# Router logits on fp32r passes turned by VectorE, and attention rows turned through DRAM

## Chip, cores and metric

The kernel runs on one core of one Trainium2 chip. The time is the device time of one execution in microseconds, the median of three runs.

## What is computed

A block of the macaron kind: a half-weighted mixture of experts, linear attention without softmax, and the same mixture again. The input is 4 sequences of 1024 rows of 128 values.

```python
x = L0_attn_x
x = x + 0.5 * ffn(layernorm(x))      # router, 16 experts of 128, top 4 of the best 2 groups, 2 shared experts
x = x + attention(layernorm(x))      # 32 heads of 4, group norm over each head and sequence, output matrix
x = x + 0.5 * ffn(layernorm(x))      # same weights as the first

logits = x_flat @ router_w.T                       # 16 logits a row
scores = sigmoid(logits); s = scores + bias        # choice by s, weights by scores
h = einsum('td,edf->etf', x, gate_w); u = einsum('td,edf->etf', x, up_w)
y = einsum('etf,efd->etd', silu(h) * u, down_w)
routed = einsum('etd,te->td', y, combine)
```

All of it is float32.

## The kernel before

**Steps and units.** The 4096 rows are cut into 8 blocks of 512, and each goes through the mixture twice: 16 steps. A step has 18 units (2 shared experts and 16 routed ones), and two steps form a pair, unrolled as `pair(p, ...)` on each engine, with `u` from 0 to 35, `w = u % 18` the place in the step and `s = u // 18` the half. Pairs 2 to 5 (steps 4 to 11) also carry the attention of one sequence each, as small pieces (`attention_stage(u, b)`) hung onto given units. Semaphores order the engines; each engine works off its own queue in order.

**One unit.** A product in float32 accuracy is made of three passes in fp32r (`product`, L509 to L516): high part of the weights times high part of the rows, low times high, high times low. A unit is three such products: gateP, upP, and yP for the unit four places earlier, so nine passes with 512 columns. ScalarE then applies silu to gateP in place (L902), VectorE multiplies it by the routing weight CB into T (L1239) and that by upP into A (L1270), ScalarE rounds A to A_hi (L876), and GpSimd forms A_lo = A - A_hi (L396). gateP and upP have two banks each: TensorE may write gateP of unit n+2 only when T of unit n is there (`gate_left`, L256), and upP when A of unit n is there.

**The next step's rows.** The normalised rows XN of step t+2 are stored to DRAM (`store_rows`), loaded in 32x32 squares into XB (`load_squares`), and at place 16 VectorE turns each square (`turn_rows`, L1153), which gives XT, the rows' transpose. XT_hi is rounded by ScalarE at place 1 (`next_high`), XT_lo is formed by GpSimd at place 2 (`next_low`), and TensorE needs both at place 0 of the next step.

**Router.** At place 1 of step t TensorE forms the logits of step t+1 in full float32: four matmuls with 128 columns of XT as the weights and the 16 columns of RT moving (`logits`, L540 to L556), into backP, with the rows on the partitions. VectorE's `route` follows in eight parts at places 2 to 9, with `route_silu` on ScalarE at place 3. `next_stats` on VectorE is at place 1, the turning of the output (`turn_output`) at place 5, of the weights at place 10. SP stores them and loads them again as CB, spread over the partitions (`load_weights`). ScalarE copies the finished sum yP to YT at place 4 (`copy_y`) before TensorE begins the next sum.

**Attention.** XA holds the normalised rows of a sequence (ScalarE, units 5 to 8). At unit 9 TensorE forms XA'XA (L571) and transposes four tiles of XA into backP, at unit 14 the other four (L585); ScalarE copies them to XAT at units 10 and 15 (L846). XAT is used at unit 33, as the weights of the last product. Small products and VectorE's work on them lie between, at units 11 to 32.

Of the kernel before, what the change touches and what calls it, by code (L numbers as in the profile page):

```python
# [34 lines left out]
P = 128  # L35
# [13 lines left out]
def macaron_kernel(nc, x, Wqkv_w, Wqkv_b, gn_w, gn_b, out_w, out_b, router_w, bias,  # L49
# [23 lines left out]
    ATT_ACT = 11  # L73
# [7 lines left out]
    with ctx:  # L81
# [63 lines left out]
        RT = sb("RT", [P, E])  # L145
        ebias = sb("ebias", [P, E])
# [21 lines left out]
        XAT = sb("XAT", [P, BT, P])  # L168
# [11 lines left out]
        quad = sb("quad", [P, P])  # L180
# [10 lines left out]
        Bm = P1  # L191
        brow = Mf
# [13 lines left out]
        y_rows = nc.dram_tensor("y_rows", [STEPS, BLOCK, P], F32, kind="Internal").ap()  # L206

# [17 lines left out]
        logits_done, silu_route, route_seq = sem("logits_done"), sem("silu_route"), sem("route_seq")  # L225
        norm_seq = sem("norm_seq")
# [11 lines left out]
        xa_ready = sem("xa_ready")  # L238
        attended = sem("attended")
# [29 lines left out]
        def _(sp):  # L269
# [78 lines left out]

            def store(t):
# [35 lines left out]
        def _(pool):  # L385
# [66 lines left out]
            def pair(p, first, attention, last):  # L452
                n = PAIR * p
                for u in range(PAIR):
                    w, s = u % UNITS, u // UNITS
                    early = first and s == 0
                    if early and u in SPLIT_AT:
                        split_low(SPLIT_AT[u])
                    if first and u == 24:
# [5 lines left out]
                    if w == 2 and not early and not (last and s == 1):  # L465
# [43 lines left out]
        def _(pe):  # L509
# [30 lines left out]
            def logits(t):  # L540

                pe.wait_ge(xt_ready, t + 1)
                if t >= 1:

                    pe.wait_ge(route_seq, ROUTE_OPS * (t - 1) + 2)
# [4 lines left out]
                if t % 2 == 0 and 0 <= b < BATCH:  # L550

                    pe.wait_ge(att_act, ATT_ACT * b + 5)
# [11 lines left out]
            def attention_stage(u, b):  # L564
# [9 lines left out]
                if u in (9, 14):  # L574

                    g = (u - 9) // 5
                    if g == 0:

                        pe.wait_ge(attended, 2 * (b + 1))
                        pe.wait_ge(route_seq, ROUTE_OPS * (2 * (b + ATT0) + 1) + 2)  # L580
                    else:

                        pe.wait_ge(att_act, ATT_ACT * b + 2)
                    for j in range(TILES):
                        mm = pe.transpose(backP[:, j * P:(j + 1) * P], XA[:, g * TILES + j, 0:P], ident[:, :])  # L585
                    mm.then_inc(att_pe, 1)
                if u == 14:

                    pe.wait_ge(att_act, ATT_ACT * b + 4)
# [12 lines left out]
                if u == 21:  # L602
                    pe.wait_ge(att_act, ATT_ACT * b + 7)
# [9 lines left out]
                if u == 30:  # L613
                    pe.wait_ge(att_act, ATT_ACT * b + 10)
                    pe.matmul(attP[:, 0:P], ATs[:, :], WoT[:, :], start=True, stop=True)  # L615
                    pe.matmul(attP[:, P:2 * P], zb[:, :], WoT[:, :], start=True, stop=True).then_inc(att_pe, 1)
                if u == 33:
                    pe.wait_ge(att_act, ATT_ACT * b + 11)
                    for g, bank in enumerate((attP, backP)):
                        if g == 0:  # L620
# [144 lines left out]
        def _(act):  # L765
# [56 lines left out]
            def attention_stage(u, b):  # L822
# [10 lines left out]
                if u == 10:  # L833
                    act.wait_ge(att_pe, 12 * b + 1)
# [8 lines left out]
                if u in (10, 15):  # L843
                    g = (u - 10) // 5
                    act.wait_ge(att_pe, 12 * b + 2 + g)
                    act.copy(XAT[:, g * TILES:(g + 1) * TILES, :], backP[:, :]).then_inc(att_act, 1)  # L846
                if u == 20:
                    act.wait_ge(att_pe, 12 * b + 6)
# [549 lines left out]
```

## Time and profile before

| | |
|---|---|
| median of 3 runs | 654.15 us (654.02 to 654.58) |
| profiled execution | 654.32 us, its span 652.6 us |
| TensorE busy | 646.5 us, 99% |
| TensorE weight loads busy | 536.4 us, 82% |
| VectorE busy | 527.4 us, 81% |
| ScalarE busy | 400.2 us, 61% |
| GpSimd busy | 464.1 us, 71% |
| granted TensorE clock | full through the whole span |

A row in order of time shows the start, the duration, the engine, the line, the operation, what it writes and what it reads, the shape and how many instructions were merged; in brackets stands the idle time of the engine before it. Matmuls are pipelined: 0.39 us is the length of one, not the distance between two. The span begins at 0; step t's place w lies at unit 18t + w. Steps 4 and 5 form the first attention pair.

### The profile page before, as it was taken

How to read it: one execution, taken by the hardware profiler on the slowest of the kernel's cores; microseconds unless marked ns; L12 is line 12 of the kernel's file. 1: busy time of each engine (PE TensorE's matmuls, PEld its weight loads, DVE VectorE, ACT ScalarE, POOL GpSimd, SP SyncE). 2: the span in 40 equal slices, each digit the busy share in tenths (PEclk: the TensorE clock that was granted, in tenths of full speed). 3: DMA queues.
4: the chain of work that ended last, by engine and by line, in shares of the span. 5: the costliest groups of instructions: out<-in, count | busy, mean ns of one | idle time of the engine just before them, and what ended most of it. 6: DMA issues, size and time to landing. Idle time of an engine off the chain costs nothing.

```text
span 652.6 us, 10128 instructions
## 1 busy us (share of the span) xinstructions
PE 646.5 (99%) x3043; PEld 536.4 (82%) x3043; DVE 527.4 (81%) x1468; ACT 400.2 (61%) x790; POOL 464.1 (71%) x400
## 2 busy tenths in 40 slices
PE   8999999999999999999999999999999999999997
PEld 7888888888888888888888888888878888888886
DVE  6898879797886979879798788897887978778674
ACT  4876656566675556755658556585565656655554
POOL 6997776777866678566785667866678677767664
PEclk9999999999999999999999999999999999999999
DMA  8726352816236162271532814528146282633510
GB/s 235 273 61 260 88 237 51 275 33 198 95 82 244 33 181 113 62 264 33 157 138 50 274 22 124 198 49 264 43 104 225 49 262 63 190 125 101 203 32 33
DMA packets 107542, 90.07 MB, mean 138 GB/s; under 512 B 67408, under 2 KB 89824, under 8 KB 107488
## 3 DMA queue, kind: packets, MB, share of 16 engines
q1 hardware_dynamic: 107488, 89.43, 43.5%
q8 instruction: 24, 0.39, 0.2%
q14 instruction: 30, 0.25, 0.1%
HBM read 79.45 MB, written 9.96 MB: 137 GB/s over the span
## 4 chain that ended last, share of the span: by engine, by line
PE 98%; DVE 1%; issue 0%; ACT 0%; POOL 0%; DVEq 0%; POOLq 0%
PE gateP L512 10%; PE yP L516 10%; PE yP L512 10%; PE yP L513 10%; PE upP L512 10%; PE gateP L516 10%; PE upP L516 10%; PE gateP L513 10%; PE upP L513 10%; PE backP L554 2%; PE attP L571 1%; PE yP L639 1%; PE attP L624 1%; PE backP L624 1%; PE backP L585 1%; PE attP L615 0%
## 5 line engine op out<-in xcount | busy, mean ns | idle before, releaser
L396 POOL TENSOR_TENSOR A_lo<-A,A_hi 128x512 fp32r<-128x512 f32 x287 | 370.7, 1293 | 171.5 <-ACT A_hi L876 170.8
L902 ACT ACTIVATE gateP<-gateP 128x512 f32<-128x512 f32 x252 | 146.5, 581 | 178.4 <-PE gateP L516 177.6
L1239 DVE TENSOR_TENSOR T<-gateP,CB 128x512 f32<-128x512 f32 x252 | 172.9, 686 | 83.4 <-ACT gateP L902 81.5
L876 ACT CAST A_hi<-A 128x512 fp32r<-128x512 f32 x287 | 176.3, 614 | 28.9 <-DVE A L1270 24.2
L1270 DVE TENSOR_TENSOR A<-upP,T 128x512 f32<-128x512 f32 x254 | 175.7, 692 | 8.7
L512 PE MATMUL gateP<-XT_hi,W_hi 128*128 128x512 f32 x288 | 117.5, 408 | 0.0
L512 PE MATMUL yP<-A_hi,W_hi 128*128 128x512 f32 x288 | 112.5, 391 | 0.0
L516 PE MATMUL yP<-A_lo,W_hi 128*128 128x512 f32 x288 | 112.4, 390 | 0.0
L516 PE MATMUL gateP<-XT_lo,W_hi 128*128 128x512 f32 x288 | 112.4, 390 | 0.0
L513 PE MATMUL gateP<-XT_hi,W_lo 128*128 128x512 f32 x288 | 112.3, 390 | 0.0
L513 PE MATMUL yP<-A_hi,W_lo 128*128 128x512 f32 x288 | 112.1, 389 | 0.0
L512 PE MATMUL upP<-XT_hi,W_hi 128*128 128x512 f32 (+1 forms) x286 | 111.7, 391 | 0.0
L516 PE MATMUL upP<-XT_lo,W_hi 128*128 128x512 f32 (+1 forms) x286 | 111.4, 389 | 0.0
L513 PE MATMUL upP<-XT_hi,W_lo 128*128 128x512 f32 (+1 forms) x286 | 111.2, 389 | 0.0
L512 PEld LDWEIGHTS upP<-XT_hi,W_hi 128*128 128x128 f32 x286 | 53.7, 188 | 13.4 <-DVE A L1270 1.9
L516 PEld LDWEIGHTS gateP<-XT_lo,W_hi 128*128 128x128 f32 x288 | 54.1, 188 | 11.8
L512 PEld LDWEIGHTS gateP<-XT_hi,W_hi 128*128 128x128 f32 x288 | 54.2, 188 | 11.5 <-DVE T L1239 1.6
L516 PEld LDWEIGHTS yP<-A_lo,W_hi 128*128 128x128 f32 x288 | 54.1, 188 | 11.5
L512 PEld LDWEIGHTS yP<-A_hi,W_hi 128*128 128x128 f32 x288 | 54.1, 188 | 11.5 <-POOL A_lo L396 0.2
L513 PEld LDWEIGHTS yP<-A_hi,W_lo 128*128 128x128 f32 x288 | 54.1, 188 | 11.2
L516 PEld LDWEIGHTS upP<-XT_lo,W_hi 128*128 128x128 f32 x286 | 53.7, 188 | 11.5
L513 PEld LDWEIGHTS upP<-XT_hi,W_lo 128*128 128x128 f32 x286 | 53.7, 188 | 10.8
(225 smaller groups left out, 627.8 us busy)
## 6 DMA issues: line engine op xcount, KB each, us to landing
CB<-combT SPq DMA_DIRECT2D x126, 512.0 KB, 6.8
y_rows<-YB SPq DMA_DIRECT2D x60, 64.0 KB, 1.9
YP<-y_rows SPq DMA_DIRECT2D x15, 256.0 KB, 2.8
x_rows<-XN SPq DMA_DIRECT2D x13, 256.0 KB, 2.3
XB<-x_rows SPq DMA_DIRECT2D x52, 64.0 KB, 2.3
out_dram<-X SPq DMA_DIRECT2D x7, 256.0 KB, 5.0
X<-in_L_attn_x_dram SPq DMA_DIRECT2D x3, 512.0 KB, 9.5
W_in<-in_L_ffn_gate_w_dram SPq DMA_DIRECT2D x4, 256.0 KB, 4.8
```

Of the source, the lines that this page charges most:

```text
L396: pool.tensor_tensor(A_lo[:, slot, :], A[:, slot, :], A_hi[:, slot, :].bitcast(F32), ALU.subtract).then_inc(low_done, 1)
L512: pe.matmul(dst, hi_w, hi_x, start=start, stop=False)
L513: pe.matmul(dst, lo_w, hi_x, start=False, stop=False)
L516: return pe.matmul(dst, hi_w, lo_x, start=False, stop=stop)
L554: mm = pe.matmul(backP[:, j * E:(j + 1) * E], XT[:, j * P:(j + 1) * P], RT[:, :], start=True, stop=True)
L571: mm = pe.matmul(attP[:, 0:P + 1], XA[:, j, 0:P], XA[:, j, :], start=(j == 0), stop=(j == BT - 1))
L585: mm = pe.transpose(backP[:, j * P:(j + 1) * P], XA[:, g * TILES + j, 0:P], ident[:, :])
L624: mm = pe.matmul(bank[:, j * P:(j + 1) * P], XAT[:, g * TILES + j, :], Bm[:, :], start=True, stop=True)
L876: act.copy(A_hi[:, v % SLOTS, :], A[:, v % SLOTS, :]).then_inc(high_done, 1)
L902: act.activation(dst, gateP[u % 2][:, :], ACT.Silu).then_inc(silu_done, 1)
L1239: dve.tensor_tensor(T[:, u % TS, :], silu, weights, ALU.mult).then_inc(gate_weighted, 1)
L1270: dve.tensor_tensor(A[:, u % SLOTS, :], bank[:, :], gated, ALU.mult).then_inc(mul_done, 1)
```

## The change

The router's matrix is split into a high and a low part once, RT4, with 128 columns: four copies of the 16 experts, each with its two parts side by side. In steps 2 to 15 RT4 is TensorE's weights, and XT_hi and then XT_lo move past it, 512 columns each, summed in backP. The result has (copy, expert, part) on the partitions and the rows along the free axis. A new `turn_logits` on VectorE at place 1 turns it: four transpositions of 32x128, each out of one group of 32 partitions and the tiles' matching 32 columns, and a sum over the two parts into prepP, from which `route` goes on. Because the logits now read XT_hi and XT_lo, `next_high` and `next_low` move to place 0, ahead of A_hi and A_lo. Steps 0 and 1 keep the old logits.

The transposes of XA leave TensorE and the copies leave ScalarE. SP stores XA to DRAM and loads it in 32x32 squares into a part of W_in, which is free by then, and VectorE turns each half of it at units 29 and 30 into XAT, another part of W_in. The other lines adapt counts (ATT_ACT, ATT_PE) and let quad share Gn's place.

```diff
+        RT4 = sb("RT4", [P, P // SQUARE, E, 2], F32R)
...
+            def store_attention_rows(b):
+                sp.wait_ge(xa_ready, b + 1)
+                sp.dma_start(xa_rows[b].rearrange("(j p) d -> p j d", p=P),
+                             XA[:, :, 0:P]).then_inc(xa_stored, 16)
...
+                squares = xa_rows[b].rearrange("(m c) (b r) -> b c m r", c=SQUARE, r=SQUARE)
+                for i in range(P // SQUARE):
+                    sp.dma_start(XAB[i * SQUARE:(i + 1) * SQUARE, :].rearrange("c (m r) -> c m r", r=SQUARE),
+                                 squares[i]).then_inc(xa_in, 16)
...
                 turn_output(t - 1)
+                attention = t % 2 == 0 and ATT0 <= t // 2 < ATT1
+                if attention:
+                    store_attention_rows(t // 2 - ATT0)
                 if t + 2 < STEPS:
                     store_rows(t + 2)
                 if t + 1 < STEPS:
                     spread_weights(t + 1)
                 if t + 2 < STEPS:
                     load_squares(t + 2)
+                if attention:
+                    load_attention_squares(t // 2 - ATT0)
                 if t + 1 < STEPS:
                     load_weights(t + 1)
...
+                    if first and u == 13:
+
+                        pool.wait_ge(router_split, 1)
+                        pool.tensor_tensor(RT4[:, :, :, 1], RT[:, :].unsqueeze(1).broadcast_to([P, P // SQUARE, E]),
+                                           RT4[:, :, :, 0].bitcast(F32), ALU.subtract).then_inc(router_split, 1)
...
-                    if w == 2 and not early and not (last and s == 1):
+                    if w == 0 and not early and not (last and s == 1):
                         next_low(2 * p + s + 1, (s + 1) % 2)
...
-                for j in range(TILES):
-                    mm = pe.matmul(backP[:, j * E:(j + 1) * E], XT[:, j * P:(j + 1) * P], RT[:, :],
-                                   start=True, stop=True)
-                mm.then_inc(logits_done, 1)
+                router = RT4[:, :, :, :].rearrange("p a e i -> p (a e i)")
+                pe.wait_ge(xt_hi_ready, t + 1)
+                pe.matmul(backP[:, :], router, XT_hi[:, t % 2, :], start=True, stop=False)
+                pe.wait_ge(xt_lo_ready, t + 1)
+                pe.matmul(backP[:, :], router, XT_lo[:, t % 2, :], start=False, stop=True).then_inc(logits_done, 1)
...
-                    for j in range(TILES):
-                        mm = pe.transpose(backP[:, j * P:(j + 1) * P], XA[:, g * TILES + j, 0:P], ident[:, :])
-                    mm.then_inc(att_pe, 1)
...
-                    act.copy(XAT[:, g * TILES:(g + 1) * TILES, :], backP[:, :]).then_inc(att_act, 1)
...
+                    if w == 0 and not first and not (last and s >= 1):
+                        next_high(t0 + s + 1, (s + 1) % 2)
...
-                        if w == (6 if early else 1):
-                            next_high(t0 + s + 1, (s + 1) % 2)
+                        if first and u in (6, UNITS):
+                            next_high(s + 1, (s + 1) % 2)
...
+            def turn_logits(t):
+
+                dve.wait_ge(logits_done, t + 1)
+                for a in range(P // SQUARE):
+                    group = slice(a * SQUARE, (a + 1) * SQUARE)
+                    own = backP[group, :].rearrange("p (j a c) -> p a j c", j=TILES, c=SQUARE)[:, a]
+                    ins = dve.transpose(lgT[group, :].rearrange("p (j c) -> p j c", c=SQUARE), own)
+                ins.then_inc(logits_turned, 1)
+                dve.wait_ge(logits_turned, t - 1)
+                dve.tensor_reduce(prepP[:, 0:TILES * E], lgT[:, :].rearrange("p (k i) -> p k i", i=2), AX.X,
+                                  ALU.add).then_inc(logits_summed, 1)
...
+                if u in (29, 30):
+                    g = u - 29
+                    dve.wait_ge(xa_in, 64 * (b + 1))
+                    dve.transpose(XAT[:, g * TILES:(g + 1) * TILES, :].rearrange("p j d -> p (j d)"),
+                                  XAB[:, g * BLOCK:(g + 1) * BLOCK]).then_inc(xat_ready, 1)
...
+                        if w == 1 and not early:
+                            turn_logits(t0 + s + 1)
```

## Rows read from the trace of the kernel before

**Rows 1.** The page: the chain that ended last, shares by engine.

```profile
PE 98%; DVE 1%; issue 0%; ACT 0%; POOL 0%; DVEq 0%; POOLq 0%
```

**Rows 2.** In order of time: start, duration, instruction; places 1 to 3 of step 4.

```profile
164.74 0.39 PE L512 MATMUL gateP<-XT_hi,W_hi 128*128 128x512 f32 x1
...
166.42 0.67 DVE L1270 TENSOR_TENSOR A<-upP,S 128x512 f32<-128x512 f32 x1
...
166.78 0.96 PE L554 MATMUL backP<-RT,XT 128*128 128x16 f32 x8
...
167.59 0.49 PE L512 MATMUL gateP<-XT_hi,W_hi 128*128 128x512 f32 x1
...
169.20 0.69 DVE L1239 TENSOR_TENSOR T<-gateP,CB 128x512 f32<-128x512 f32 x1 [0.64 <-ACT gateP L902]
...
169.77 0.39 PE L512 MATMUL gateP<-XT_hi,W_hi 128*128 128x512 f32 x1
...
169.93 0.69 DVE L1270 TENSOR_TENSOR A<-upP,T 128x512 f32<-128x512 f32 x1
...
170.53 0.22 DVE L1058 TENSOR_SCALAR near<-backP 128x64 f32<-128x64 f32 x1
...
172.77 0.68 DVE L1239 TENSOR_TENSOR T<-gateP,CB 128x512 f32<-128x512 f32 x1
```

**Rows 3.** In order of time, step 3: T of 3.2, T of 3.6, gateP of 3.8.

```profile
131.53 0.69 DVE L1239 TENSOR_TENSOR T<-gateP,CB 128x512 f32<-128x512 f32 x1 [1.27 <-ACT gateP L902]
...
140.46 0.68 DVE L1239 TENSOR_TENSOR T<-gateP,CB 128x512 f32<-128x512 f32 x1
...
142.30 0.39 PE L512 MATMUL gateP<-XT_hi,W_hi 128*128 128x512 f32 x1
```

**Rows 4.** In order of time, step 4: T of 4.6 and gateP of 4.8.

```profile
179.38 0.68 DVE L1239 TENSOR_TENSOR T<-gateP,CB 128x512 f32<-128x512 f32 x1
...
180.12 0.50 PE L512 MATMUL gateP<-XT_hi,W_hi 128*128 128x512 f32 x1
```

**Rows 5.** In order of time, step 5: places 1, 2, 7, 9 and 12.

```profile
208.10 0.68 DVE L1270 TENSOR_TENSOR A<-upP,S 128x512 f32<-128x512 f32 x1
...
208.48 0.96 PE L554 MATMUL backP<-RT,XT 128*128 128x16 f32 x8
...
209.73 0.48 PE L512 MATMUL gateP<-XT_hi,W_hi 128*128 128x512 f32 x1
...
211.32 0.69 DVE L1239 TENSOR_TENSOR T<-gateP,CB 128x512 f32<-128x512 f32 x1 [1.66 <-ACT gateP L902]
...
224.05 0.68 DVE L1239 TENSOR_TENSOR T<-gateP,CB 128x512 f32<-128x512 f32 x1
...
224.78 0.50 PE L512 MATMUL gateP<-XT_hi,W_hi 128*128 128x512 f32 x1
...
233.79 0.69 DVE L1239 TENSOR_TENSOR T<-gateP,CB 128x512 f32<-128x512 f32 x1 [0.73 <-ACT gateP L902]
```

**Rows 6.** Waits: who waited for whom, us in total, times, longest.

```profile
PEld gateP L512 <- DVE T L1239: 1.6, 4, 0.4
```

**Rows 7.** The chain that ended last, in order of time: place 9 of step 4.

```profile
186.38 0.44 PE backP L585 x4
```

**Rows 8.** Groups by line: count, busy us, mean ns of one, idle time before.

```profile
L420 POOL TENSOR_TENSOR XT_lo<-XT,XT_hi 128x512 fp32r<-128x512 f32 x14 | 18.2, 1298 | 0.0
...
L1158 DVE STREAM_TRANSPOSE XT<-XB 128x512 f32<-128x512 f32 x13 | 9.1, 702 | 0.0
...
L1099 DVE TENSOR_REDUCE prepP<-ahead 128x16 f32<-128x128 f32 x16 | 4.7, 295 | 0.5
...
L1145 DVE STREAM_TRANSPOSE CTB<-comb 128x64 f32<-128x64 f32 x14 | 3.3, 235 | 0.0
```

**Rows 9.** SP's queue in order of time, step 4; the page's issues of XB.

```profile
193.66 10.97 SPq L319 DMA_DIRECT2D CB<-combT  x8
...
XB<-x_rows SPq DMA_DIRECT2D x52, 64.0 KB, 2.3
```

More of the change, by code:

```diff
@@ L72, in macaron_kernel @@
     ATT_OPS = 18
-    ATT_ACT = 11
+    ATT_ACT = 9
+    ATT_PE = 10
     assert D == P and BT * P == SEQ and NBLK == 2 * BATCH and E == GROUPS * PER_GROUP
@@ L167, in macaron_kernel @@
         XA = sb("XA", [P, BT, P + 1])
-        XAT = sb("XAT", [P, BT, P])
+        lgT = sb("lgT", [P, P])
         GS = sb("GS", [P, P + 1])
@@ L191, in macaron_kernel @@
         Bm = P1
+        quad = Gn
+        XAB = W_in[:, 0:3, :, :].rearrange("p u i d -> p (u i d)")[:, 0:BT * P]
+        XAT = W_in[:, 3:6, :, :].rearrange("p u i d -> p (u i) d")[:, 0:BT, :]
         brow = Mf
@@ L206, in macaron_kernel @@
         y_rows = nc.dram_tensor("y_rows", [STEPS, BLOCK, P], F32, kind="Internal").ap()
+        xa_rows = nc.dram_tensor("xa_rows", [BATCH, SEQ, P], F32, kind="Internal").ap()
         x_first, x_rest = sem("x_first"), sem("x_rest")
@@ L238, in macaron_kernel @@
         xa_ready = sem("xa_ready")
+        xa_stored, xa_in, xat_ready = sem("xa_stored"), sem("xa_in"), sem("xat_ready")
         attended = sem("attended")
@@ L347, in load_squares, with load_attention_squares @@
                                  squares[b]).then_inc(rows_in, 16)
+            def store_attention_rows(b):
+                sp.wait_ge(xa_ready, b + 1)
+                sp.dma_start(xa_rows[b].rearrange("(j p) d -> p j d", p=P),
+                             XA[:, :, 0:P]).then_inc(xa_stored, 16)
+            def load_attention_squares(b):
+                sp.wait_ge(xa_stored, 16 * (b + 1))
+                if b == 0:
+                    sp.wait_ge(w_lo_done, UNITS)
+                else:
+                    sp.wait_ge(xat_ready, 2 * b)
+                squares = xa_rows[b].rearrange("(m c) (b r) -> b c m r", c=SQUARE, r=SQUARE)
+                for i in range(P // SQUARE):
+                    sp.dma_start(XAB[i * SQUARE:(i + 1) * SQUARE, :].rearrange("c (m r) -> c m r", r=SQUARE),
+                                 squares[i]).then_inc(xa_in, 16)
             def store(t):
@@ L540, in logits @@
             def logits(t):
-                pe.wait_ge(xt_ready, t + 1)
-                if t >= 1:
-                    pe.wait_ge(route_seq, ROUTE_OPS * (t - 1) + 2)
+                if t < 2:
+                    pe.wait_ge(xt_ready, t + 1)
+                    if t == 1:
+                        pe.wait_ge(route_seq, 2)
+                    for j in range(TILES):
+                        mm = pe.matmul(backP[:, j * E:(j + 1) * E], XT[:, j * P:(j + 1) * P], RT[:, :],
+                                       start=True, stop=True)
+                    mm.then_inc(logits_done, 1)
+                    return
+                if t == 2:
+                    pe.wait_ge(router_split, 2)
+                    pe.wait_ge(route_seq, ROUTE_OPS + 2)
+                else:
+                    pe.wait_ge(logits_turned, t - 2)
                 b = (t - 1) // 2 - ATT0
@@ L573, in attention_stage @@
                     mm.then_inc(att_pe, 1)
[L574 to L583, printed above, removed]
-                    for j in range(TILES):
-                        mm = pe.transpose(backP[:, j * P:(j + 1) * P], XA[:, g * TILES + j, 0:P], ident[:, :])
-                    mm.then_inc(att_pe, 1)
                 if u == 14:
-                    pe.wait_ge(att_act, ATT_ACT * b + 4)
+                    pe.wait_ge(att_act, ATT_ACT * b + 3)
                     pe.matmul(attP[:, 0:P], GS[:, 0:P], WvT[:, :], start=True, stop=True)
@@ L905, in pair @@
                             split_high(unit)
+                    if first and u == 6:
+                        act.wait_ge(setup_sb, 1)
+                        act.copy(RT4[:, :, :, 0], RT[:, :].unsqueeze(1).broadcast_to([P, P // SQUARE, E])
+                                 ).then_inc(router_split, 1)
                     if first and u == 20:
@@ L1052, in route @@
                 if part == 0:
-                    dve.wait_ge(logits_done, t + 1)
-                    flat = backP[:, 0:TILES * E]
+                    if t < 2:
+                        dve.wait_ge(logits_done, t + 1)
+                        flat = backP[:, 0:TILES * E]
+                    else:
+                        dve.wait_ge(logits_summed, t - 1)
+                        flat = prepP[:, 0:TILES * E]
                     near_f = near[:, :, :].rearrange("p t e -> p (t e)")
```

38 lines of the change are left out of this document (17 added, 21 removed).

## The prediction

> **What bounds the kernel now.** I read the chain that ended last first: it lies on TensorE for 98% of the span [rows 1]. So time is won only by taking slots out of TensorE's queue, and lost only where another engine makes it wait. Then the instructions in order of time. Units are named step.place: 4.6 is place 6 of step 4. A unit is nine passes of 128x512; in 4.1 they begin at 164.74 and what follows them at 166.78 [rows 2], so a unit takes 2.04 us and a pass 0.227 of the queue (its shown 0.39 overlaps its neighbours).
>
> Next the reader should see how near VectorE is. T of 4.2 starts at 169.20, A at 169.93, and A ends at 170.62 [rows 2]: with the gaps a unit takes 1.45 us of VectorE and leaves it 0.59 of 2.04 for everything else. TensorE may not write gateP of unit n+2 before T of unit n is done (gate_left). In step 3, T of 3.6 ends at 141.14 and gateP of 3.8 starts at 142.30, so 1.16 is in hand [rows 3]. In step 4, the first half of an attention pair, T of 4.6 ends at 180.06 and gateP of 4.8 starts at 180.12 [rows 4]: nothing is in hand. In step 5, T of 5.7 ends at 224.73 and gateP of 5.9 starts at 224.78 [rows 5]: nothing either. The waits agree: TensorE's weight loads waited for T four times, once for each attention pair [rows 6].
>
> **What leaves TensorE.** The eight logit matmuls of 128x16 (two records for each of four) take from 166.78 to 167.59, and the unit behind them takes 169.77 - 167.59 = 2.18 in place of 2.04 [rows 2]: 0.81 + 0.14 = 0.95. Two passes of the kind that all units consist of replace them, 0.45, which saves 0.50. Steps 2 to 15 are concerned, so place 1 of steps 1 to 14: six steps without attention (1, 2, 3, 12, 13, 14), four first halves (4, 6, 8, 10) and four second halves. In a second half fp32 matmuls of the attention follow the logits, the slow unit stays and 0.35 is saved. Four transposes of XA take 0.44 [rows 7]; they leave at places 9 and 14, 0.88 in each first half. If nothing waited, the sum would be 6 x 0.50 + 4 x 0.50 + 4 x 0.35 + 4 x 0.88 = 9.9 us.
>
> **What VectorE gets.** turn_logits stands ahead of next_stats, of the attention's statistics and of T of place 2; all of that queues behind its wait, and TensorE behind T. A of 4.1 ends at 167.09. The second new pass starts at 164.74 + 10 x 0.227 = 167.01 and takes 0.39 [rows 2], so the logits are there at 167.40, a wait of 0.31. Then come four transpositions of 32x128. One of 64 columns takes 0.235 and one of 512 takes 0.702 [rows 8]; on that line 128 columns take 0.235 + 64 x 0.00104 = 0.30. How closely the four follow each other isn't in the trace: no instruction of VectorE there works on other partitions than its neighbour. The bounds: overlapping by 0.09, as A does, which ends at 170.62, with what starts at 170.53 [rows 2], they take 4 x 0.21, some 0.89 with the last one's tail; one after the other with 0.04 between, as from T to A of 4.2 [rows 2], they take 4 x 0.34 = 1.36. The pairwise sum that waits for them is like the reduction of 0.295 [rows 8], less such an overlap: 0.21. So turn_logits costs 1.10 or 1.57 behind its wait. I take 1.57: the four write four different groups of partitions, and every overlap in the trace is between instructions on the same ones.
>
> The Trainium skill sides with the long end: "VectorE: DVE Perf Modes", section "Two Vector instructions with no wait between them", says that an instruction whose operands begin in another quadrant of 32 partitions than those before it starts only when all earlier ones have finished. By it the sum is the one with 1.57, without it the one with 1.10. No row here shows it.
>
> **First halves.** From the end of A of 4.1 to T of 4.2 VectorE had 2.11 us, 0.64 of it idle [rows 2], so 1.47 of work. After the change T of 4.2 starts at 167.40 + 1.57 + 1.47 = 170.44, later than 169.20 by 1.24. From there to T of 4.6 VectorE gives nothing back: 2.15 us pass from A of 4.2 to T of 4.3 [rows 2] where a unit leaves 0.59, and the router's parts go on. So TensorE is held at gateP of 4.8 until 1.2 later than before, whatever it saved ahead of it. It will also wait at place 4, since copy_y stands behind A_hi and route_silu in ScalarE's queue, but that lies within the same 1.2. Then it saves 0.88 at places 9 and 14. Net +0.33 each, +1.3 for four.
>
> **Second halves.** The logits of step 5 start at 208.48; + 0.227 + 0.39 they are there at 209.10. A of 5.1 ends at 208.78 and T of 5.2 starts at 211.32 after 1.66 of idle time, so next_stats takes 0.88. With 1.57 and 0.88, T starts at 211.55, behind a gateP that moves from 209.73 to 209.38 [rows 5]: 2.17 behind it in place of 1.59. Places 2 to 5 give VectorE about what a unit leaves, so none pays it back; place 6 adds 1.07 for dev2, and T of 5.7 is about 0.7 later behind its gateP, with 0.05 in hand. A stall of 0.68, less 0.35: +0.33 each, +1.3 for four.
>
> **Other steps.** VectorE idles 1.27 before T of 3.2 [rows 3]. The new work is 0.31 + 1.57 = 1.88 and gateP comes 0.36 earlier, so T falls back by 0.97 behind its gateP; by another 0.14 as the next unit is no longer slow, and by some 0.15 that VectorE idled up to T of 3.6. That is 1.25 where 1.16 is in hand: a stall of 0.1 at place 8, one as large at place 12, and 0.15 at place 4, where copy_y comes after two pieces that follow A of place 2. So 0.35 of the 0.50 goes again. Five steps save 0.15 each. Step 1 saves nothing, where ScalarE still copies XT first and XT_lo comes late. Together -0.75.
>
> **Edits at no cost.** XT_hi and XT_lo move to place 0, ahead of A_hi and A_lo. gateP of 4.0 is whole about 163.6; silu and XT_hi take 0.6 each and XT_lo 1.30 [rows 8], so it is there about 166.1, where the second pass asks for it at 167.01; if it weren't, each logit would wait up to 1.3. A_lo is formed over a unit ahead of its use and bears that. ScalarE loses two copies of XAT, for which nobody waited. VectorE's two transpositions of XAT take 0.702 each [rows 8] less the overlap. They fall to 5.11, where VectorE idles 0.73 before T of 5.12 [rows 5], and to 5.12, where T of 5.13 comes some 0.5 later, far less than the 1.2 in hand in a unit without attention; with no cover they would cost 5 us. On SP's queue the four loads of squares stand ahead of the CB loads, which began at 193.66 and the first of which is wanted by T of 5.2 at 211.32 [rows 5, 9]. The present squares, half as large, land in 2.3 us [rows 9]; the new ones take some 9 of 17 even if each waits for the one before it. XA's store is issued in SP's wait for the normalised rows. The router's two splits are an instruction each in step 0.
>
> **Sum.** 1.3 + 1.3 - 0.75 = +1.85 us. The profiled execution took 654.32 (span 652.6), the median is 654.15; on the median 656.0, slower by 0.28%.
>
> **Rivals.** (a) The four transpositions overlap, 1.10 in all. T of 4.2 is then 0.77 late: first halves 0.74 - 0.88 = -0.14, second halves a stall of 0.25 and -0.1, other steps -0.48: together -3.9, so 650.3. For it: small instructions overlap throughout. Against it: the different partitions. From the forecast to it each 0.1 of turn_logits is 1.2 us of the kernel, so below 1.42 the kernel is faster than before. (b) The waits at 4.8 and 5.9 aren't VectorE's doing, and all 9.9 us are won: 644.3. Against it stand the 0.06 and 0.05 us. (c) A transposition of 128 columns out of PSUM takes 0.075 more than the line says, 0.3 more at each of 14 steps: 659.7. The trace turns only SBUF; but T and A read PSUM and take 0.69, no more than is usual for their size. (d) Something between (a) and the forecast, within 0.2% of before.
>
> **Chances.** Forecast 0.50 (653.5 to 658.5; a fifth of it within 0.2%), (a) 0.20, (b) 0.07, (c) 0.10, (d) 0.13. A measurement of this kernel tells 0.2% (1.3 us) from no change. Faster 0.27, same 0.23, slower 0.50. The range takes in (a) and most of (c): 650.3 to 659.5.
>
> **What would show it.** Right: two logit passes of 0.23 with no slow unit behind; four records of about 0.30 with starts 0.34 apart on VectorE; T of 4.2 some 1.6 us later behind its gateP; TensorE's waits for T grown from 1.6 us to several, at places 8 and 9 of attention steps. Wrong: starts of the four 0.21 apart, waits for T as before, CB or XAT waited for, or XT_lo waited for at each logit.

## The result, and the profile of the changed kernel

The changed kernel takes 656.35 us (median of 7 runs, 656.21 to 656.91). The kernel before, timed beside it, takes 654.16 (7 runs, 653.95 to 654.58). The ratio is 1.0033, 95% interval 1.0022 to 1.0045: slower by 2.2 us, outside the noise of the runs. The forecast was 656.0 and slower by 0.28%.

| | before | after |
| --- | --- | --- |
| profiled execution, us | 654.32 | 656.27 |
| its span, us | 652.6 | 654.5 |
| TensorE busy, us and share of the span | 646.5, 99% | 642.6, 98% |
| TensorE's weight loads waiting for T, us | 1.6 [rows 6] | 7.3 |

The page of the changed kernel: the line of the span, the busy times, and the shares of the chain that ended last, which answer to [rows 1].

```profile
span 654.5 us, 9988 instructions
...
PE 642.6 (98%) x2927; PEld 522.1 (80%) x2927; DVE 554.5 (85%) x1546; ACT 396.9 (61%) x783; POOL 465.0 (71%) x401
...
PE 84%; DVE 12%; issue 2%; POOL 1%; DMA 1%; ACT 1%; SPq 0%; DVEq 0%; ACTq 0%
```

The share of VectorE in the chain went from 1% to 12%. TensorE's busy share, 99% before and 98% now, hardly shows it, as each stall is a few tenths of a microsecond in a step of 42. So I read the waits next. The columns are engine, tile and line, what it waited for, us in total, times, longest.

```profile
PEld gateP L547 <- DVE T L1298: 7.3, 12, 1.0
PEld yP L547 <- ACT YT L819: 3.7, 8, 0.7
...
PE gateP L547 <- DVE T L1298: 2.8, 7, 0.6
PEld attP L640 <- DVE chmean L1254: 2.7, 4, 0.7
...
PEld attP L632 <- DVE Mm L1248: 2.1, 4, 0.5
...
PEld backP L602 <- POOL XT_lo L450: 0.5, 1, 0.5
```

The first line answers to [rows 6]: 4 waits with 1.6 us became 12 with 7.3. YT, chmean and Mm are new among the waits of this size; the forecast has the first and not the other two. XT_lo, which now stands ahead of the logits, was waited for once.

Then the instructions in order of time (start, duration, engine and line, operation; in brackets the idle time ahead and what ended it), places 0 to 5 of step 4. They answer to [rows 2].

```profile
163.89 1.29 POOL L450 TENSOR_TENSOR XT_lo<-XT,XT_hi 128x512 fp32r<-128x512 f32 x1 [0.74 <-ACT XT_hi L844]
...
165.54 0.67 DVE L1329 TENSOR_TENSOR A<-upP,S 128x512 f32<-128x512 f32 x1
...
165.91 0.39 PE L600 MATMUL backP<-XT_hi,RT 128*128 128x512 f32 x1
...
166.14 0.39 PE L602 MATMUL backP<-XT_lo,RT 128*128 128x512 f32 x1
...
166.37 0.40 PE L547 MATMUL gateP<-XT_hi,W_hi 128*128 128x512 f32 x1
...
166.57 1.29 DVE L1092 STREAM_TRANSPOSE lgT<-backP 32x128 f32<-32x128 f32 x4 [0.35 <-PE backP L602]
...
167.90 0.29 DVE L1095 TENSOR_REDUCE prepP<-lgT 128x64 f32<-128x128 f32 x1
...
168.10 0.17 DVE L1050 TENSOR_REDUCE prepP<-bst 128x8 f32<-128x16 f32 x1
...
168.43 0.39 PE L547 MATMUL gateP<-XT_hi,W_hi 128*128 128x512 f32 x1
...
169.57 0.67 DVE L1298 TENSOR_TENSOR T<-gateP,CB 128x512 f32<-128x512 f32 x1
...
172.32 0.50 PE L547 MATMUL yP<-A_hi,W_hi 128*128 128x512 f32 x1 [0.31 <-ACT YT L819]
...
173.12 0.68 DVE L1298 TENSOR_TENSOR T<-gateP,CB 128x512 f32<-128x512 f32 x1
...
173.86 0.50 PE L547 MATMUL gateP<-XT_hi,W_hi 128*128 128x512 f32 x1 [0.57 <-DVE T L1298]
```

The reader should see four things. The two logit passes cost 166.37 - 165.91 = 0.46, where the fp32 logits took 0.81 [rows 2], and the unit behind them takes 168.43 - 166.37 = 2.06 instead of 2.18. VectorE waits 0.35 for them and turns for 168.10 - 166.57 = 1.53. T of 4.2 starts 3.20 behind its gateP (169.57 - 166.37) instead of 1.61 (169.20 - 167.59, [rows 2]). And TensorE pays at 4.5 already: its gateP begins at 173.86, right behind T of 4.3, with 0.57 idle. In the kernel before it began at 173.85, in a step that started 0.87 later, so all that had been gained is gone.

To see where the time goes, one number for each step is enough: the length of the step in us, from its first gateP pass at place 0 to that of the next step, from the trace in order of time.

| steps | before | after | difference |
| --- | --- | --- | --- |
| first halves (4, 6, 8, 10), mean | 41.61 | 41.97 | +0.36 each |
| second halves (5, 7, 9, 11), mean | 41.63 | 42.19 | +0.56 each |
| 2, 3, 12, 13, mean | 37.67 | 37.46 | -0.21 each |
| 14 | 37.68 | 37.20 | -0.48 |
| 1 | 38.15 | 38.02 | -0.13 |

4 x 0.36 + 4 x 0.56 - 4 x 0.21 - 0.48 - 0.13 = +2.2 us, which is the whole of the difference between the medians.

### The profile page after: what moved, and what is told of

Read it like the earlier page. It is cut to its first block, busy times and chain, and to the rows that moved or that the text cites. A ratio compares the mean times of both kernels' runs of the same rounds, so it can differ in the third digit from the quotient of the medians.

```text
span 654.5 us, 9988 instructions
## 1 busy us (share of the span) xinstructions
PE 642.6 (98%) x2927; PEld 522.1 (80%) x2927; DVE 554.5 (85%) x1546; ACT 396.9 (61%) x783; POOL 465.0 (71%) x401
## 4 chain that ended last, share of the span: by engine, by line
PE 84%; DVE 12%; issue 2%; POOL 1%; DMA 1%; ACT 1%; SPq 0%; DVEq 0%; ACTq 0%
PE gateP L547 9%; PE gateP L551 9%; PE upP L547 9%; PE gateP L548 9%; PE upP L551 9%; PE upP L548 9%; PE yP L551 9%; PE yP L547 9%; PE yP L548 9%; DVE T L1298 2%; DVE A L1329 2%; DVE lgT L1092 1%; PE attP L617 1%; DVE ast L1220 1%; PE backP L659 1%
## 5 line engine op out<-in xcount | busy, mean ns | idle before, releaser
L551 PEld LDWEIGHTS yP<-A_lo,W_hi 128*128 128x128 f32 x288 | 54.1, 188 | 11.4
```

What stands on the lines that cost most here:

```text
L551: return pe.matmul(dst, hi_w, lo_x, start=False, stop=stop)
```

## Experiments

The theory: turn_logits takes 1.57 us of VectorE ahead of T, and T holds TensorE at the places where nothing was in hand before; the four groups of partitions are what makes the turning long. The rivals: the attention part pays for it (squares, CB or XAT late), ScalarE's order at place 4 is the wait that decides, or it is the move of XT_lo.

### One part alone

**attention_only** keeps the attention rows turned through DRAM and has the router's fp32 matmuls of before.

```diff
-                    if w == 0 and not early and not (last and s == 1):
+                    if w == 2 and not early and not (last and s == 1):
                         next_low(2 * p + s + 1, (s + 1) % 2)
...
-                pe.matmul(backP[:, :], router, XT_hi[:, t % 2, :], start=True, stop=False)
-                pe.wait_ge(xt_lo_ready, t + 1)
-                pe.matmul(backP[:, :], router, XT_lo[:, t % 2, :], start=False, stop=True).then_inc(logits_done, 1)
+                for j in range(TILES):
+                    mm = pe.matmul(backP[:, j * E:(j + 1) * E], XT[:, j * P:(j + 1) * P], RT[:, :],
+                                   start=True, stop=True)
+                mm.then_inc(logits_done, 1)
...
-                        if w == 1 and not early:
-                            turn_logits(t0 + s + 1)
```

> Only the attention's part of the change: XA goes through DRAM and VectorE turns it; the router, XT_hi and XT_lo stay as before. Theory (VectorE's turning of the logits is what costs): TensorE saves 4 x 0.88 us and nothing else moves, about 650.6 us, 3.5 below before. Rival (the new transfers, or VectorE's two transpositions at places 11 and 12, cost something): above 652.

Measured: 650.57 us (650.49 to 651.04), 0.9943 of before (0.993 to 0.9957). First halves take 40.74, which is 0.87 less than before's 41.61; second halves 41.63 and the others 37.67 are as before. That is the 4 x 0.88 of the forecast, and nothing of it is given back: VectorE's two transpositions into XAT in each pair, at 5.11 and 5.12, and the loads of squares are hidden behind TensorE's work. The waits for T are exactly those of [rows 6]:

```profile
PEld gateP L542 <- DVE T L1267: 1.6, 4, 0.4
```

**logits_only** is the other half: the router by two passes and turning, and the attention rows turned by TensorE and copied by ScalarE as before.

```diff
+                if u in (9, 14):
+                    g = (u - 9) // 5
...
+                    for j in range(TILES):
+                        mm = pe.transpose(backP[:, j * P:(j + 1) * P], XA[:, g * TILES + j, 0:P], ident[:, :])
+                    mm.then_inc(att_pe, 1)
...
+                if u in (10, 15):
+                    g = (u - 10) // 5
...
+                    act.copy(XAT[:, g * TILES:(g + 1) * TILES, :], backP[:, :]).then_inc(att_act, 1)
```

> Only the router's part; XA is transposed by TensorE and copied by ScalarE as before. Theory: what the whole change gives less the attention's saving, 656.35 + 3.5 = 659.9 us. If the two parts disturb each other (transfers against queues), it is nearer to 656.

Measured: 660.21 us (659.85 to 660.46), 1.0089 of before (1.0075 to 1.0103). First halves take 42.85, 1.24 more than before; second halves 42.18, 0.55 more; 2, 3, 12 and 13 some 0.2 less (one of them as before), step 14 37.20. The parts add up: -3.6 and +6.0 make +2.4, and together they make +2.2. So the attention part is a gain of 3.6 us in itself, and the router part a loss of 6. A first half's 1.24 is the lateness of T of place 2, with nothing gained back. The 0.55 of a second half holds something else too, shown further down.

### What makes the turning long

**one_turn** replaces the four transpositions by one of 128x128.

```diff
-                for a in range(P // SQUARE):
-                    group = slice(a * SQUARE, (a + 1) * SQUARE)
-                    own = backP[group, :].rearrange("p (j a c) -> p a j c", j=TILES, c=SQUARE)[:, a]
-                    ins = dve.transpose(lgT[group, :].rearrange("p (j c) -> p j c", c=SQUARE), own)
+                ins = dve.transpose(lgT[:, :], backP[:, 0:P])
```

> The whole change, but one transposition of 128x128 in the place of the four of 32x128, so that the router sees wrong logits for most rows; VectorE's work at place 1 falls by 1.0 us, TensorE's is untouched. Theory (VectorE's time at place 1 carries to the places where TensorE has nothing in hand): about 1.0 less in each first half, 0.8 in each second half and 0.3 in the other steps, 8 to 9 us less than the change, about 648. Rival (the cost lies in the order of ScalarE's and GpSimd's queues at place 0): 655 or more.

Measured: 649.07 us (648.96 to 650.11), 0.9922 of before (0.991 to 0.9935). The row of the group by line (count, busy us and mean ns of one, idle time before):

```profile
L1089 DVE STREAM_TRANSPOSE lgT<-backP 128x128 f32<-128x128 f32 x14 | 4.4, 312 | 3.4 <-PE backP L602 3.0
```

One transposition over all four groups takes 312 ns, as much as each of the four over one group. It frees about 1.0 us of VectorE at each of 14 steps and gives 656.35 - 649.07 = 7.3 us. The first halves fall from 41.97 to 40.98, by the whole 0.99, the second halves from 42.19 to 41.60, by 0.59, and steps 2, 3, 12 and 13 from 37.46 to 37.20. So VectorE's time at place 1 goes one for one into the length of a first half, and by some 0.6 for each 1.0 into that of a second half. (The profiled execution took 650.11, 1.04 above the median, and 0.86 of it lies in step 1, where T of place 2 waited 1.89 for CB.)

**same_group** keeps four transpositions with the same number of elements, but each reads and writes partitions 0 to 31.

```diff
                 for a in range(P // SQUARE):
-                    group = slice(a * SQUARE, (a + 1) * SQUARE)
-                    own = backP[group, :].rearrange("p (j a c) -> p a j c", j=TILES, c=SQUARE)[:, a]
-                    ins = dve.transpose(lgT[group, :].rearrange("p (j c) -> p j c", c=SQUARE), own)
+                    own = backP[0:SQUARE, :].rearrange("p (j a c) -> p a j c", j=TILES, c=SQUARE)[:, a]
+                    ins = dve.transpose(free[0:SQUARE, a * P:(a + 1) * P].rearrange("p (j c) -> p j c", c=SQUARE), own)
```

> The whole change, but all four transpositions read and write the first 32 partitions, into four separate places, and the sum over pairs reads memory that holds no logits: the routing is meaningless, the number and size of instructions is the same. If different partitions are what keeps the four apart, they now start about 0.23 us apart instead of 0.33 and the kernel gains some 3 us, 653. If a transposition out of PSUM never overlaps with the next, they stay 0.33 apart and the time is that of the change, 656.4.

Measured: 652.43 us (652.06 to 652.75), 0.9971 of before (0.996 to 0.9982). In order of time, place 1 of step 4:

```profile
166.67 0.90 DVE L1095 STREAM_TRANSPOSE W_in<-backP 32x128 f32<-32x128 f32 x4 [0.35 <-PE backP L602]
...
167.60 0.29 DVE L1098 TENSOR_REDUCE prepP<-W_in 128x64 f32<-128x128 f32 x1
...
167.80 0.17 DVE L1050 TENSOR_REDUCE prepP<-bst 128x8 f32<-128x16 f32 x1
```

The group by line, first of same_group and then of the changed kernel:

```profile
L1095 DVE STREAM_TRANSPOSE W_in<-backP 32x128 f32<-32x128 f32 x56 | 12.5, 272 | 3.4 <-PE backP L602 3.0
```

```profile
L1092 DVE STREAM_TRANSPOSE lgT<-backP 32x128 f32<-32x128 f32 x56 | 17.5, 312 | 4.0 <-PE backP L602 3.0
```

The four take 0.90 and the next instruction starts 0.93 behind the first; over four groups they take 1.29 and it starts 1.33 behind (167.90 - 166.57). The whole of turn_logits is 1.13 against 1.53. They lie close to the two bounds that the prediction set, 1.10 and 1.57. The difference decides the sign: 0.40 us of VectorE, 14 times, moves the kernel from 2.2 slower to 1.8 faster than before (654.20 beside it), and each of the two is more than the 1.3 us that a measurement can tell. The rule of the Trainium skill that the prediction weighed ("VectorE: DVE Perf Modes", "Two Vector instructions with no wait between them") agrees with both rows: where neighbours lie in different quadrants, the starts are 0.33 apart for an instruction of 0.312, so each waits for the one ahead, and where they lie in the same one the starts are 0.21 apart for 0.272.

### ScalarE's order at place 4

YT was waited for 3.7 us. The forecast called that wait covered. **copy_first** moves route_silu behind copy_y, so that YT comes earlier.

```diff
                         copy_y(t0 + s - 1)
+                        if not (last and s >= 1):
+                            route_silu(t0 + s + 1)
...
-                        if w == (9 if early else 3):
+                        if early and w == 9:
                             route_silu(t0 + s + 1)
```

> The whole change with one order altered on ScalarE: in steps 1 to 14 route_silu comes right behind copy_y instead of ahead of it, so TensorE's wait for YT at place 4 goes. If that wait lies within the delay that VectorE imposes anyway, as the prediction says, first halves don't change and the total falls by 0.2 us at most, 656.1. If it comes on top, 0.7 us in each of four first halves and a little elsewhere are won, 653.4.

Measured: 656.64 us (656.22 to 656.85), 1.0033 of before (1.0021 to 1.0046), the same as the changed kernel. The waits:

```profile
PEld gateP L547 <- DVE T L1300: 8.0, 12, 1.2
...
PE gateP L547 <- DVE T L1300: 3.4, 7, 0.7
...
PEld yP L547 <- ACT YT L819: 2.4, 4, 0.6
```

The waits of weight loads and matmuls for YT fell from 3.7 + 1.2 to 2.8 us, those for T rose from 7.3 + 2.8 to 11.4, and the lengths of the steps are the same to 0.02 (41.96, 42.19, 37.46). A wait in the list isn't a cost: here it stood ahead of another that ended at the same time whatever became of the first.

### Where the second halves lose

Second halves lose 0.56 each, not 0.33, and TensorE waits for Mm and chmean there, two results of the attention's work on VectorE. In order of time, places 0 and 1 of step 5 and the end of place 5, of the changed kernel:

```profile
205.95 1.30 POOL L450 TENSOR_TENSOR XT_lo<-XT,XT_hi 128x512 fp32r<-128x512 f32 x1 [0.98 <-ACT XT_hi L844]
...
207.20 2.59 POOL L426 TENSOR_TENSOR A_lo<-A,A_hi 128x512 fp32r<-128x512 f32 x2
...
207.40 1.25 DVE L1248 TENSOR_TENSOR Mm<-Mf,blk 128x128 f32<-128x128 f32 x1
...
208.57 0.68 DVE L1329 TENSOR_TENSOR A<-upP,S 128x512 f32<-128x512 f32 x1
...
209.17 1.28 DVE L1092 STREAM_TRANSPOSE lgT<-backP 32x128 f32<-32x128 f32 x4
...
218.11 0.38 PE L640 MATMUL attP<-chmean,blkm 128*128 128x1 f32 x2 [0.22 <-DVE chmean L1254]
```

Mm is a product of 128x128 and takes 1.25 us. Before, it took 0.29:

```profile
L1194 DVE TENSOR_TENSOR Mm<-Mf,blk 128x128 f32<-128x128 f32 x4 | 1.2, 291 | 0.1
```

It begins 0.20 after GpSimd's A_lo and ends at 208.65; the first of the two A_lo, at 1.30 each, ends at 208.50. In the kernel before GpSimd had no XT_lo at place 0, and no subtraction ran beside Mm. The same goes for attention_only, where XT_lo stays at place 2 and Mm takes 0.29; in logits_only, one_turn, same_group and copy_first, where XT_lo is at place 0, it takes 1.25. The suspicion: VectorE is held until GpSimd's instruction is over. **mm_from_psum** leaves GpSimd alone and changes only from where VectorE reads: Mf lies in PSUM, so Mm has one operand in SBUF instead of two.

```diff
-                    dve.scalar_tensor_tensor(Mf[:, :], rv[:, :], bk[:, :], attP[:, 0:P],
+                    dve.scalar_tensor_tensor(attP[:, P:2 * P], rv[:, :], bk[:, :], attP[:, 0:P],
                                              ALU.mult, ALU.add).then_inc(att_seq, 1)
                     dve.wait_ge(att_seq, v + 11)
-                    dve.tensor_tensor(Mm[:, :], Mf[:, :], blk1[:, :], ALU.mult).then_inc(att_seq, 1)
+                    dve.tensor_tensor(Mm[:, :], attP[:, P:2 * P], blk1[:, :], ALU.mult).then_inc(att_seq, 1)
```

> The whole change, but the attention's product Mm = Mf * mask reads Mf from PSUM instead of SBUF. In the change it takes 1.25 us in each second half instead of 0.29, ending exactly with GpSimd's subtraction that began before it. Theory: VectorE with two operands in SBUF waits for GpSimd, and XT_lo's move to place 0 put it in the way. Then Mm takes 0.3 again, VectorE begins the transpositions of step 5 about 0.5 us earlier, and each second half wins 0.5: 654.2. If the time has another cause, or nothing depends on it, 656.4.

Measured: 654.17 us (654.03 to 654.75), 0.9998 of before (0.999 to 1.0007). Step 5 in order of time:

```profile
207.10 2.54 POOL L426 TENSOR_TENSOR A_lo<-A,A_hi 128x512 fp32r<-128x512 f32 x2
...
207.30 0.29 DVE L1248 TENSOR_TENSOR Mm<-attP,blk 128x128 f32<-128x128 f32 x1
...
207.51 0.68 DVE L1329 TENSOR_TENSOR A<-upP,S 128x512 f32<-128x512 f32 x1
...
208.55 1.29 DVE L1092 STREAM_TRANSPOSE lgT<-backP 32x128 f32<-32x128 f32 x4 [0.36 <-PE backP L602]
```

GpSimd's pair lies where it lay, also beginning 0.20 ahead of Mm, and Mm takes 0.29. The turning starts 0.62 earlier, 0.11 of it because the whole step does, and waits for TensorE again (0.36) instead of for VectorE's own queue. Second halves fall from 42.19 to 41.68: 4 x 0.51 = 2.0 of the 2.2 us. One product that waits for another engine costs as much as the whole of the regression; without it the change makes no difference that these runs can measure.

The 0.51 has two parts. The distance from gateP of 5.1 to that of 5.2 falls from 3.23 to 2.87 us, by 0.36, and that from gateP of 5.5 to 5.6, with the wait for chmean in it, from 2.67 to 2.55. The wait for chmean itself stays:

```profile
PEld attP L640 <- DVE chmean L1254: 2.1, 4, 0.5
```

In one_turn it is gone, and the distance is the 2.18 of the kernel before, though Mm still takes 1.25 there. So the wait for chmean comes mostly from turn_logits, which stands ahead of the attention's work in VectorE's queue, and only to a small part from Mm.

### Two kernels faster than both

one_turn says what a single transposition is worth. **groups32** gets it with the whole computation: the router's weights, 16 columns doubled to 32, are multiplied in fp32 four times, each into its own 32 partitions, and move the 128 rows that belong there. The result has the form that one 128x128 transposition turns, and there is nothing to sum. The splits go back to their old places; the attention part of the change stays.

```diff
-                pe.matmul(backP[:, :], router, XT_hi[:, t % 2, :], start=True, stop=False)
-                pe.wait_ge(xt_lo_ready, t + 1)
-                pe.matmul(backP[:, :], router, XT_lo[:, t % 2, :], start=False, stop=True).then_inc(logits_done, 1)
+                pe.wait_ge(xt_ready, t + 1)
+                rows4 = XT[:, :].rearrange("p (j a c) -> p a j c", j=TILES, c=SQUARE)
+                for a in range(P // SQUARE):
+                    mm = pe.matmul(backP[a * SQUARE:(a + 1) * SQUARE, 0:P],
+                                   RT2[:, :, :].rearrange("p i e -> p (i e)"), rows4[:, a], start=True, stop=True)
+                mm.then_inc(logits_done, 1)
...
+                ins = dve.transpose(lgT[:, :], backP[:, 0:P])
```

> Another way to the same logits: the router stays in full float32, 32 columns wide (the 16 experts twice), and four matmuls move those 128 rows whose results are to lie in one group of 32 partitions, into that group; one transposition of 128x128 on VectorE turns them, with no sum over pairs, and XT_hi and XT_lo stay at their old places. The attention's part is that of the change. VectorE gets 0.32 us at place 1 instead of 1.53. By the theory it then delays nothing (T of 4.2 could start at 169.2, as before), first halves win 0.88, the others the 0.37 by which four matmuls of 128 columns (0.11 each) are shorter than the eight: about 7 us, 647. If VectorE's turning isn't the cause, it stays above 650.6, the time of the attention's part alone.

Measured: 647.9 us (647.78 to 648.01), 0.9902 of before (0.9888 to 0.9916). In order of time, place 1 of step 4:

```profile
165.44 0.43 PE L596 MATMUL backP<-XT,RT 128*32 128x128 f32 x8
...
165.94 0.32 DVE L1083 STREAM_TRANSPOSE lgT<-backP 128x128 f32<-128x128 f32 x1 [0.28 <-PE backP L596]
...
166.18 0.15 DVE L1044 TENSOR_REDUCE prepP<-bst 128x8 f32<-128x16 f32 x1
```

The logits in full fp32 take 0.43 in place of 0.96 [rows 2]. gateP of 4.1 starts at 163.31 and gateP of 4.2 at 165.80, 2.49 apart: a unit of 2.04, 0.09 until the first logit matmul starts, and 0.36 for the logits. The unit behind them takes 2.18 again. That is 0.09 + 0.36 + 0.14 = 0.59 of TensorE, against 0.46 + 0.02 = 0.48 for the two passes and 0.95 before, and the steps without attention bear it out: 0.36 shorter than before. The turning takes 0.24 (166.18 - 165.94) instead of 1.53. First halves take 40.75, second halves 41.49, the others 37.31.

**groups32_psum** adds what the last two experiments taught: Mm reads PSUM, and so does dev2, a single column that took 1.07 us in every kernel so far, and route_silu stands behind copy_y.

```diff
+                    devp = attP[:, 3 * P + 1:3 * P + 2]
+                    dve.tensor_tensor(devp, chmean[:, :], attP[:, 2 * P:2 * P + 1], ALU.subtract)
...
-                    dve.scalar_tensor_tensor(dev2[:, :], dev[:, :], dev[:, :], chvar[:, :],
+                    dve.scalar_tensor_tensor(dev2[:, :], devp, dev[:, :], chvar[:, :],
```

> The one before, and besides Mm and dev2 read PSUM (dev2 took 1.07 us for one column in every second half, at the place where TensorE has nothing in hand) and route_silu comes behind copy_y. Theory: 0.9 us of VectorE's at place 6 of second halves go, and TensorE's waits at places 8 to 10 there shrink by some 0.2 to 0.3 each: about 1 us less than groups32, 646. If dev2's time cost nothing, the two are equal.

Measured: 646.27 us (645.96 to 646.62), 0.9877 of before (0.9864 to 0.9891), 8.1 us less than the kernel before in the same call (654.35). The page's shares of the chain that ended last (they are the same in groups32, and were 84% and 12% in the changed kernel), and dev2's group by line:

```profile
PE 97%; DVE 2%; issue 0%; ACT 0%; POOL 0%; DVEq 0%; POOLq 0%
```

```profile
L1257 DVE SCALAR_TENSOR_TENSOR dev<-attP,dev,chvar 128x1 f32<-128x1 f32 x4 | 0.9, 219 | 0.1
```

dev2 went from 1.07 to 0.22, beside a subtraction that began 0.29 before it and ran on for 0.79 behind it, and the second halves from 41.49 to 40.99: 4 x 0.50 = 2.0, where the medians differ by 1.6. Of the 0.50, 0.20 is won by gateP of places 9 and 10, where T of 5.7 had 0.05 in hand [rows 5], and 0.29 at place 12. There TensorE waited for zb, which ScalarE forms at the end of the chain of small steps that follows dev2; the wait stands in groups32 and, with the same numbers, in the kernel before, and in groups32_psum it is gone:

```profile
PEld attP L644 <- ACT zb L885: 1.7, 4, 0.4
```

Mm has no part in it, since it takes 0.29 in groups32 too. The order of route_silu gained nothing in copy_first; no run parts it from dev2 here.

## Why the prediction was right, and where it was not

**The size of turn_logits: right.** It measures 1.53; the forecast took 1.57, with 1.10 as the other bound, and same_group shows that the groups of partitions make the difference, not the number or the size of the instructions. Within it two terms were off and cancelled: a transposition takes 0.312, not 0.30, and the starts lie 0.33 apart, not 0.34. Rival (c) (0.075 more for each) is out by that 0.312. The wait ahead was 0.35, said 0.31. Rival (a), all overlapping, is what same_group does: it gave 652.43 against its 650.3, and half of the distance lies in the second halves, 41.81 long or +0.17 where (a) had -0.1: four times 0.27. Mm takes 1.25 in that run as well, and (a) knew of it no more than the forecast did.

**First halves: right, +0.36 each for +0.33.** T of 4.2 came 1.24 later from the start of its step, as worked out, and gateP of 4.8 1.22 later (its start went from 180.12 [rows 4] to 180.47 while its step starts 0.87 earlier). Places 9 and 14 gave 0.45 and 0.43 back. logits_only, without the latter, shows 1.24. What was wrong is the place: TensorE is first held at 4.4 and 4.5, by YT and T of 4.3, not at 4.8. It was still 1.2 in all, because the hold runs on from unit to unit and the last one sets it. The waits for YT lie within it, as said; copy_first shows that.

**Second halves: mechanism right in part, +0.56 for +0.33, and a step failed.** The forecast had a saving of 0.35 at place 1 and a stall of 0.68 behind it, most of it at place 9. Measured: gateP of 5.2 starts at 209.17, 0.56 earlier than before [rows 5] in a step that starts 0.50 earlier, so 0.06 was saved; gateP of 5.6 was late by another 0.52 (from 0.56 to 0.04 earlier), behind the wait for chmean, and gateP of 5.9 by only 0.10. The step that failed is "Edits at no cost". For the move of XT_lo it asked only whether XT_lo is there in time and whether A_lo bears it. It didn't ask whom GpSimd would then meet on VectorE. Mm took 1.25 instead of 0.29, and mm_from_psum takes 0.51 a step off, 0.36 at place 1 and the rest mostly at place 5. Without Mm's hold the second halves are +0.05 (41.68 against 41.63): 0.43 saved at place 1, 0.37 lost at place 5 and some 0.1 behind it. So the forecast for them was too high but for that hold, and its place was wrong too: it followed T to place 9 and left out that the attention's own small results, chmean first, stand behind turn_logits in the same queue and are waited for earlier. Its 0.68 isn't what its terms give either: T later by 2.17 - 1.59 = 0.58, less the 0.05 in hand, is 0.53, and no row stands behind the other 0.15. The 1.07 of dev2 can't be it, as it was there in the kernel before.

**Steps without attention: -0.21 each for -0.15.** T of 3.6 ends at 141.11 and gateP of 3.8 starts at 141.22, so 0.11 is in hand where it was 1.16 [rows 3]; the forecast had used up all of it and 0.1 more. The rows, in order of time, step 3 of the changed kernel:

```profile
140.43 0.68 DVE L1298 TENSOR_TENSOR T<-gateP,CB 128x512 f32<-128x512 f32 x1
...
141.22 0.44 PE L547 MATMUL gateP<-XT_hi,W_hi 128*128 128x512 f32 x1
```

In step 3 gateP starts 0.03 late at place 5, 0.02 at 6, 0.12 at 9 and 0.06 at 10; the forecast had 0.15 at place 4 and 0.1 each at 8 and 12. Step 14 gained 0.48: it belongs to the last pair, which has no next_stats, so VectorE had room. That was a difference between steps that I passed over when I wrote "five steps save 0.15". Step 1 gained 0.13 for 0. In all -1.45 for the -0.75 of the sum.

**The total** was near by luck, because two misses cancel: for the second halves the forecast had 0.9 too little of a loss, for the other steps 0.7 too little of a gain. The forecast 656.0 stands 0.35 from the 656.35; its terms stand up to 0.9 off. Two sums of the rivals don't come out as written: 14 times 0.3 is 4.2 and puts (c) at 660.2, not 659.7, and 0.47 less of turn_logits leaves 0.77 and 0.21 in (a), not 0.74 and 0.25. Nothing in the argument hangs on either.

**The other edits at no cost: right.** attention_only gives the full 3.5 us of the transposes, so the squares, the two turnings of XAT and the later CB loads are hidden. In the changed kernel XAT (the trace calls it W_in) is not among what TensorE waits for. XT_lo was there in time: at 165.18 for a pass at 166.14, and waited for once in the kernel, 0.5. Rival (b), that VectorE doesn't hold TensorE, is out by the 7.3 us of waits and by one_turn.

**Open.** Why the first halves of groups32 (40.75) are no shorter than those of attention_only (40.74), though 0.36 leaves TensorE at places 1 and 2, wasn't tried by itself. T of 4.2 starts 6.50 behind the start of its step in attention_only and 6.36 in groups32, and from there to T of 4.6 VectorE waits for nobody in either (10.18 and 10.34 us; the 0.16 is near, which takes 0.38 instead of 0.21). So T of 4.6 stands at 16.68 and 16.70, and what TensorE gains ahead of it is held back again. That is an argument from rows, not a run.

## What to carry to other kernels

When TensorE waits for VectorE at even one place of a stage, price an edit by what it adds to VectorE's queue ahead of that place, not by what it takes from TensorE: here 0.40 us on VectorE, by the choice of partitions alone, decided the sign. A step that is moved must be checked against whatever runs on the other engines at its new place, down to where their operands lie. And before spreading one small job over four instructions, look for the form in which the producer already leaves the data for one.

## What the runs showed of the hardware

**VectorE can be held by GpSimd until GpSimd's instruction is over.** Mm (two operands in SBUF, 128x128) took 1.25 us beside a subtraction of GpSimd that began 0.20 before it, 0.29 when one operand lay in PSUM beside the same subtraction, and 0.29 with both in SBUF and no subtraction running. dev2, one column, took 1.07 with its operands in SBUF and 0.22 with one in PSUM, beside a running subtraction each time. In the kernel before, the two ended together:

```profile
222.82 1.29 POOL L396 TENSOR_TENSOR A_lo<-A,A_hi 128x512 fp32r<-128x512 f32 x1 [0.98 <-ACT A_hi L876]
...
223.05 1.07 DVE L1211 SCALAR_TENSOR_TENSOR dev<-dev,chvar 128x1 f32<-128x1 f32 x1
```

222.82 + 1.29 = 224.11 and 223.05 + 1.07 = 224.12. This row was in the trace of before; the prediction read "1.07 for dev2" as the cost of the instruction. For a column of 128x1 (chmean, another, takes 0.15) that should have raised the question. The Trainium skill has the rule: "GPSIMD Engine Reference", section "1. Specifications", says that GpSimd's SBUF interfaces are shared with VectorE, with contention where VectorE's instruction has two SBUF inputs or runs in a 2-port perf mode. The rows agree for two SBUF inputs.

It reaches an instruction that reads a single tile, too. near<-lgT, from SBUF to SBUF, takes 0.50 in the mean of groups32's 14, near<-backP of the two steps that read PSUM 0.22. In order of time, place 2 of step 1 and then of step 4 of groups32:

```profile
56.87 0.18 DVE L1100 TENSOR_SCALAR near<-lgT 128x64 f32<-128x64 f32 x1
...
57.42 1.29 POOL L426 TENSOR_TENSOR A_lo<-A,A_hi 128x512 fp32r<-128x512 f32 x1 [1.80 <-ACT A_hi L903]
...
167.98 1.30 POOL L426 TENSOR_TENSOR A_lo<-A,A_hi 128x512 fp32r<-128x512 f32 x1
...
168.95 0.38 DVE L1100 TENSOR_SCALAR near<-lgT 128x64 f32<-128x64 f32 x1
...
169.36 0.22 DVE L1103 SCALAR_TENSOR_TENSOR lg<-near,lgT 128x64 f32<-128x64 f32 x1
```

In step 1 GpSimd is idle, and near takes 0.18. In step 4, the same instruction on the same tile with the same stride takes 0.38 and ends at 169.33, right behind A_lo at 169.28; in each of the other 12 steps, too, it lasts until 0.05 behind the subtraction that runs beside it. So the stride isn't the cause. Whether it runs in a 2-port perf mode, which would put it under the same sentence of the skill, no row shows.

**Four fp32 matmuls of 128 columns into four groups of 32 partitions** are done in 0.43 us, eight records, with weights of 128x32. The fp32 logits of before, four matmuls with weights of 128x128 and 16 columns moving, took 0.96, also eight records. More columns moved, 512 instead of 64, and the time was halved; which of the smaller weights and the separate groups does it, these runs don't tell.
